# A fused convolution and attention kernel on one core: a second load for the first group of x, and the first pixel rows moved behind the fifth group

## What is computed

```python
t1 = p1_w * x
t2 = x + t1
t5 = _unfold(x, 3, 7, 1, 1, 1, 3)                   # 21 shifted copies of x
t7 = jnp.einsum('oc,nchw->nohw', p7_w, relu(x))
t8 = _unfold(t7, 1, 5, 1, 3, 0, 6)                  # 5 shifts along w, 3 apart
t9 = x[:, :, None] - t8
t10 = grouped 1x1 product of t2 with p10_w, 4 groups of 32 channels
t11 = jnp.einsum('nck,nmk->ncm', t1f, t5f) / math.sqrt(h * w)
t13 = jnp.einsum('ncm,nmk->nck', t11, t10) / math.sqrt(c * 21)
out = jnp.maximum(t13, t9.mean(2))
```

## Time and profile before

| | us |
|---|---|
| runs of the kernel | 390.27, 390.73, 391.36 |
| median | 390.73 |
| the profiled execution, its own time | 389.69 |
| its span, first to last instruction | 387.9 |
| PE busy in the span | 382.1 (98%) |
| DVE busy | 328.4 (85%) |
| ACT busy | 254.2 (66%) |
| POOL busy | 88.2 (23%) |

### The profile page before, as it was taken

One profiled execution on the slowest core, in us unless ns is written; L12 is line 12 of the kernel. 1 busy time (PEld: TensorE's weight loads), 2 busy tenths in 40 slices (PEclk: granted clock), 3 DMA queues, 4 the chain that ended last, 5 costly groups with the idle time before them and its releaser, 6 DMA issues.

```text
span 387.9 us, 10231 instructions
## 1 busy us (share of the span) xinstructions
PE 382.1 (98%) x4022; PEld 169.4 (44%) x4022; DVE 328.4 (85%) x401; ACT 254.2 (66%) x721; POOL 88.2 (23%) x77
## 2 busy tenths in 40 slices
PE   7999999999999999999999999999999999999996
PEld 3233563334633365333743338333383334732383
DVE  7998999899798896888968887889868889688645
ACT  3525379779567765677476772676827768377790
POOL 1634212221222202222022220222202222222300
PEclk9999999999999999999999999999999999999999
DMA  8999486583977556794677937779377773553115
GB/s 296 385 352 416 165 292 209 178 295 118 324 266 249 212 200 218 257 315 139 218 235 251 331 117 253 227 261 322 128 245 248 251 278 111 177 179 111 54 57 216
DMA packets 28704, 88.80 MB, mean 229 GB/s; under 512 B 3312, under 2 KB 3824, under 8 KB 28656
## 3 DMA queue, kind: packets, MB, share of 16 engines
q1 hardware_dynamic: 28656, 88.14, 65.9%
HBM read 71.35 MB, written 16.78 MB: 227 GB/s over the span
## 4 chain that ended last, share of the span: by engine, by line
PE 95%; DVE 2%; DMA 2%; SPq 0%; issue 0%; DVEq 0%
PE ps_y L828 41%; PE ps_y L927 13%; PE ps_t L850 12%; PE ps_p L850 12%; PE ps_y L839 8%; PE ps_t L927 2%; DMA xw<-x_conv 2%; PE ps_y L850 1%; PE ps_y L1072 1%; PE ps_t L828 1%; PE ps_y L975 1%; PE ps_p L828 1%; DVE v_planes L580 0%; PE ps_p L975 0%; DVE v_planes L575 0%; DVE v_planes L569 0%
## 5 line engine op out<-in xcount | busy, mean ns | idle before, releaser
L828 PE MATMUL ps_y<-v_planes,u_planes 64*64 64x512 f32 x1488 | 183.4, 594 | 0.9 <-DVE v_planes L575 0.7
L306 POOL TENSOR_TENSOR t1T<-t1T,p1T_sb 128x512 f32<-128x512 f32 x64 | 81.1, 1288 | 267.9 <-PE ps_y L839 236.9
L414 ACT ACTIVATE t<-xn,p_plus 128x64 f32<-128x64 f32 x512 | 127.9, 334 | 0.0
L850 PE MATMUL ps_t<-t,aT 64*64 64x512 f32 x440 | 113.0, 590 | 0.1
L850 PE MATMUL ps_p<-box,p_fifth 64*64 64x512 f32 x424 | 108.8, 589 | 0.0
L828 PEld LDWEIGHTS ps_y<-v_planes,u_planes 64*64 64x64 f32 x1488 | 55.0, 133 | 113.0 <-issue 107.8
L641 DVE STREAM_TRANSPOSE yT<-ps_y 128x512 f32<-128x512 f32 x62 | 40.7, 694 | 30.0 <-PE ps_y L839 29.8
L338 ACT ACTIVATE base<-ps_p 128x512 f32<-128x512 f32 x55 | 32.8, 597 | 47.4 <-PE ps_p L850 46.9
L927 PEld LDWEIGHTS ps_y<-t1T,yT 128*128 128x128 f32 x448 | 50.5, 192 | 5.7 <-issue 5.7
L927 PE MATMUL ps_y<-t1T,yT 128*128 128x128 f32 x448 | 51.9, 277 | 0.0
L675 DVE TENSOR_TENSOR base<-ps_t,base 128x512 f32<-128x512 f32 x56 | 38.4, 686 | 12.1 <-PE ps_t L850 11.8
(11 more groups left out here) (75 smaller groups left out, 218.9 us busy)
## 6 DMA issues: line engine op xcount, KB each, us to landing
xw<-x_conv SPq DMA_DIRECT2D x63, 561.0 KB, 6.7
xn<-x_nat SPq DMA_DIRECT2D x32, 512.0 KB, 4.5
t1T<-x_pix SPq DMA_DIRECT2D x32, 512.0 KB, 5.3
out<-base SPq DMA_DIRECT2D x63, 256.0 KB, 4.7
u_planes<-w_tiles SPq DMA_DIRECT2D x4, 336.0 KB, 5.9
out<-base SPq DMA_DIRECT2D x2, 128.0 KB, 2.0
p1T_sb<-p1T SPq DMA_DIRECT2D x1, 128.0 KB, 8.4
p_sb<-p7T SPq DMA_DIRECT2D x1, 64.0 KB, 8.3
```

Source lines behind the costliest of these rows:

```text
L306: nc.gpsimd.tensor_tensor(part, part, p1T_sb[:, e, :].unsqueeze(1).broadcast_to([P, 4, C]), ALU.mult).then_inc(t1_ready, 1)
L414: last = nc.scalar.activation(t2[:, h, W * r:W * (r + 1)], xn[:, f, at:at + W], ACT.Copy, scale=p1_plus[:, 8 * h + r:8 * h + r + 1])
L828: last = nc.tensor.matmul(dst[TILE * pair:TILE * pair + TILE, :], weights_of(rows_of(half), u, weights, TILE * k, TILE), data_of(rows_of(h ...
L850: last = nc.tensor.matmul(dst[cols, 0:data.shape[-1]], weights[rows, cols], data[rows, :], start=start, stop=False, skip_group_check=True)
```

## The change

Unit 0 gets a load of its BACK half, issued behind unit 1's two loads and ahead of the weights of group 2. V_3 of unit 0 is then made from it by one operation of 128 partitions, with a wait on the load. V_1 of unit 0 is made from the FRONT half in two operations, as before. So the count of early planes keeps its extra step for unit 0 and that of outer planes loses it (early_done and outer_done take the place of pairs_done), and the loads of buffer 0 are counted like the others (loads goes away). The loads of pixel rows 0 and 1 move from between units 3 and 4 to behind unit 4, ahead of rows 2 and 3.

```diff
-        def pairs_done(u):
-            return 2 * (u + 1) + min(u + 1, TURNED)
-        def loads(u, order):
-            return u // 3 + 1 - (order == BACK and u % 3 < TURNED)
+        def early_done(u):
+            return 2 * (u + 1) + 1
+        def outer_done(u):
+            return 2 * (u + 1)
...
                 if 3 <= u < LATE + 3:
-                    sp.wait_ge(early_ready, pairs_done(u - 3))
-                    sp.wait_ge(outer_ready, pairs_done(u - 3))
+                    sp.wait_ge(early_ready, early_done(u - 3))
+                    sp.wait_ge(outer_ready, outer_done(u - 3))
...
-                for order in range(1 if u < TURNED else 2):
+                for order in (FRONT,) if u == 0 else (FRONT, BACK):
...
             load_group(1)
+            sp.dma_start(xw[:, 0, BACK], x_conv[0, 0, BACK]).then_inc(xw_loaded[0][BACK], 16)
             load_weights(2)
...
             load_group(3)
-            load_pixels(0, 0, 2)
             load_group(4)
-            load_pixels(0, 2, 4)
+            load_pixels(0)
             load_natural(0, 1)
...
-                if u < TURNED:
+                if (u, back) == (0, V_1):
                     for half in range(2):
...
                 else:
-                    dve.wait_ge(xw_loaded[b][BACK], 16 * loads(u, BACK))
+                    dve.wait_ge(xw_loaded[b][BACK], 16 * (u // 3 + 1))
```

More of the change, by code:

```diff
@@ L32 @@
 LATE = 4
-TURNED = 1
 ZERO_ROWS = 7
@@ L320, in _ @@
             nc.gpsimd.memset(v_fourth[:, :, 0:BLOCKS_PAD:BLOCKS_PAD - 1, :], 0.0).then_inc(edges_zeroed, 1)
-            pool.wait_ge(early_ready, pairs_done(1))
+            pool.wait_ge(early_ready, early_done(1))
             weights(2)
@@ L567, in pair_of_planes @@
                 b = u % 3
-                dve.wait_ge(xw_loaded[b][FRONT], 16 * loads(u, FRONT))
+                dve.wait_ge(xw_loaded[b][FRONT], 16 * (u // 3 + 1))
                 nc.vector.tensor_tensor(inner(u, front), xw[:, b, FRONT, front == V_2, :, 0:PAIRS],
                                         first_rows(b, FRONT)[1], ALU.subtract).then_inc(ready, 1)
-                if u < TURNED:
+                if (u, back) == (0, V_1):
                     for half in range(2):
@@ L607, in planes_low @@
                     return
-                dve.wait_ge(xw_loaded[u % 3][FRONT], 16 * loads(u, FRONT))
+                dve.wait_ge(xw_loaded[u % 3][FRONT], 16 * (u // 3 + 1))
                 dve.wait_ge(m_done, u - 2 - (u < LATE + 3))
@@ L867, in one_two @@
                     if u < LATE:
-                        pe.wait_ge(early_ready, pairs_done(u))
+                        pe.wait_ge(early_ready, early_done(u))
                     else:
@@ L890, in outer_planes @@
                 if u < LATE:
-                    pe.wait_ge(outer_ready, pairs_done(u))
+                    pe.wait_ge(outer_ready, outer_done(u))
                 else:
```

## The result

The changed kernel takes 393.45 us (median of 6 runs, 392.23 to 395.61) against 390.38 us for the kernel before (6 runs): the ratio is 1.0089, with a 95% interval of 1.007 to 1.0108. By the ratio that is 3.5 us slower, by the two medians 3.1, where 3.7 were forecast; 393.45 lies inside the range of 391.9 to 395.8, 1 us under the forecast of 394.4.

A forecast was written before the change was run, and what follows sets the result against it. TensorE, without holes behind 16.40 us, was taken as the bound, so delays stay. Two waits, 4.2 or 3.2 us in all, middle 3.7, took the profiled 389.69 to 393.4; against the median 390.73, 394.4 us, range 391.9 to 395.8.

The forecast's parts named there:

- Bound and head: TensorE has no holes behind 16.40 us; up to there, its stop before unit 2 shrinks, -0.2 to 0.0, taken as -0.1 us.
- The new load: Unit 0's extra 561 KB, ahead of weights 2, land at 11.0 us; loads behind, up to unit 3, land 1.4 us later.
- Unit 3: Its two halves of x, landing at 17.5 and 18.9 us before, land at 18.9 and 20.3.
- The dry queue: DMA queue empty for some 2 us behind unit 3; unit 4's first half lands at 24.0 us, unit 5's at 34.0.
- the path that the prediction drew from there: Late x starts unit 5's low planes at 33.5 to 35 us; GpSimd's blocks then delay its V_1 and the box sums.
- The 3.3 us that the prediction worked out from the Trainium skill: Time from issue to landing of a half-unit load in an idle queue; the prediction itself used 4.2 us from the rows.
- Unit 4's V_1 itself is hit by 0.1 us at most: On VectorE, GpSimd's t1 pieces falling on unit 4's planes would delay its V_1 by no more than 0.1 us.
- The two waits at unit 5 and at the box sums: TensorE waits 1.2 us for unit 5's V_1 near 37, then 2 to 3 us at pair_first near 46 to 47; chance 0.66.
- The sum: Total TensorE delay of 4.2 or 3.2 us, first wait included, middle 3.7 taken; the head's -0.1 not added.
- Rival 1: x in time, GpSimd's blocks falling elsewhere, box sums within 1.2 us of slack: 390.6 us; chance 0.13 with whatever stays within 0.3%.

The follow-up runs named there:

- the runs with small pieces: Changed kernel, image 0's t1 pieces on GpSimd cut to 8 of 512 columns: first four 393.29 us, ratio 1.0085; all eight 390.39 us, ratio 1.0003.
- the last version: Kernel before plus new load and one-piece V_3, GpSimd's t1 pieces 2 and 4 waiting for V_3 of units 4 and 5: 389.48 us, ratio 1.0001.

## Why the prediction was right, step by step, and where it was not

- **Bound and head.** TensorE without holes behind 16.4 us, so that each stop stays: right. The head was to win 0.1 us; the stop at unit 2 did go, 0.2 us, and the rest of the 0.44 was x landing sooner by chance. The 0.2 us come from the load and not from the edit on V_3, to which the prediction gave them: unit 2 starts 8.63 or 8.64 us behind the first product in all nine kernels with the new load, also in the one that makes V_3 in two pieces, and 8.80 to 9.14 behind it in the four without. GpSimd's weights(2) ran unblocked, 0.66 us each (0.67 in the earlier trace rows), and ACT's swap began at 14.32.
- **The new load.** Forecast to land at 11.0, landed at 11.15. VectorE's and GpSimd's rows up to seeds(0) came as worked out.
- **Unit 3, the step that failed first.** I had its second half at 20.3 by adding 1.4 to 18.9. It landed at 21.68, 2.6 us behind the first half. In all nine kernels with the new load it came 2.2 to 2.9 us behind its first half, between 20.9 and 21.7; in the four without it 1.4 or 1.5 behind. In the kernel before, pixel row 0 stood in that place and landed at 21.80, 3.0 us behind the load ahead of it. I took that for pixel row 0's own slowness and didn't ask whom it would hit next. Its cause is open. It is not only a matter of the time: with GpSimd's first piece held back in the kernel before, a load landed at 19.9 and the next at 21.3 without any delay. Nor is it a want of throughput: with the new load alone, the queue moved 392 GB/s from 19 to 21 us, and the half still landed at 21.65. It made VectorE 1.2 us late from seeds(2) on.
- **The dry queue.** Right in place and size: 64 GB/s from 19 to 21 us, unit 4 issued at 19.91 and landed at 23.6 (24.0 forecast), unit 5 at 34.51 (34.0). But the path that the prediction drew from there was not taken: in the changed kernel VectorE came to unit 5's planes 2.2 us behind the landing of their x, so that x of unit 5 set nothing. The 3.3 us that the prediction worked out from the Trainium skill for a load to an idle queue were 3.7; the skill's figure is fitted to DMAs that GpSimd issues ("DMA: Bandwidth & Descriptors", Anatomy of one DMA), and these are issued by SyncE.
- **"Unit 4's V_1 itself is hit by 0.1 us at most", the step that failed.** It held only for a VectorE on time, as the run with the pixel loads alone shows. With VectorE late, the first piece at 26.69 fell one operation earlier, on V_3 of unit 3, and three pieces instead of one came ahead of V_1. The prediction had counted only the pieces of pixel row 0 against these planes; four came in a row. The sum by the rows: 28.16, its end before, + 1.19 of lateness + 3 x 1.07 is 32.56, its end after, where TensorE wanted it at 29.0.
- **The two waits at unit 5 and at the box sums.** They did not occur in the changed kernel, since TensorE was by then as late as VectorE. With unit 4 on time they did, at 1.5 and 1.9 us with the first four pieces cut, and 0.9 and 1.9 for the pixel loads alone. The forecast for them was 1.2 and 2 to 3.
- **The sum.** 3.7 forecast, 3.5 measured. The mechanism, GpSimd's pieces between VectorE's operations, was right; the place, the path through unit 5's x and the number of waits were not, and that the sum fits all the same is luck. Six arrangements in which the pieces themselves came late (the changed kernel among them) gave 3.3 to 4.1 us, as if three to four pieces of 1.1 us always had to pass with little slack to absorb them. That is argued and not shown: with the new load alone, where only VectorE was late, it was 1.9, and with the first piece held back in the kernel before, 2.0 us of the profiled execution's loss were stop and 1.6 clock.
- **The rivals.** Rival 1 was x on time and GpSimd's blocks falling elsewhere, at -0.1. It is not what happened, but the runs with small pieces show its price: with the blocks gone the loss is 0.1 us, though x is late. Of the clock no rival had spoken. It falls behind some of the stops, in a part of the runs, and is worth up to 2.7 us: the slowest run, at 395.61, came within 0.2 us of the range's upper end by it.

## What to carry to other kernels

Before a load is moved, look at what its landing starts: here a pixel row started GpSimd work, and this work made the loss; data that came late cost 1 us at most without it. Two engines that block each other should be tied to each other's progress (GpSimd's pieces wait for VectorE's planes), and not each to a third's, or a shift of 1 us in either makes them collide. It needs room as well: with the new load alone such waits took back the whole loss, in the changed kernel, whose pixel rows land late, they took back nothing (+3.4 and +4.1 us). And an experiment that takes away one cause and leaves the time as it was has not cleared that cause: look whether the next wait has stepped into its place.

## What the runs showed of the hardware

- A piece of 128x512 on GpSimd lengthened an operation of VectorE with two operands in SBUF by 1.07 us where it got in between, and by 0.9 to 1.0 where it began inside the operation's turn (1.61 and 1.68 for 0.72, 2.17 for 1.22). Operations that read PSUM beside such pieces kept their length, 1.3 us for two transposes and 0.7 for a seed. The Trainium skill has this as an exclusive lock on a pair of ports that the two share ("SBUF — State Buffer", Who interferes with whom): the second one is blocked until the first is done. All traces here agree. What they add is that GpSimd comes in between two operations of VectorE that stand back to back, so that a row of four lost four times 1.07 us.
- TensorE's granted clock fell from 2.4 to 1.2 GHz behind a stop of 4.4 us in three of four runs, at 2.7 us each, and behind the changed kernel's stop of 3.6 us fully in one of six. In the other profiled executions it fell behind stops of 2.0 and 3.2 us and not behind those of 1.3 to 1.9. It isn't tied to these stops alone: two of twelve runs of the last version, whose trace has no stop there, had a mean clock of 0.996 too.
- A load that was issued to an almost empty queue landed after 3.7 us (561 KB, at 19.91), sooner than the 4.2 of the earlier trace rows.
